# Three small VectorE operations per attention head, moved behind the first maximum of the next head

## The reference

```
x = x + 0.5 * ffn(layernorm(x))          # ternary weights, bias, gamma, beta
x = x + attn(layernorm(x))
x = x + 0.5 * ffn(layernorm(x))

attn:  q, k, v = x @ w.T, by heads;  q, k = rope(q), rope(k)
       scores = q k^T / sqrt(32), masked (causal by blocks of 64)
       softmax over keys, times v, then @ w_o.T
```

## Time and profile before

| | |
|---|---|
| median of 3 runs | 636.81 us (636.68 to 638.52) |
| profiled execution | 636.18 us, span of the trace 634.4 us |
| TensorE matmul busy | 554.8 us (87%), 3586 matmuls |
| VectorE busy | 409.6 us (65%), 782 instructions |
| ScalarE busy | 310.5 us (49%), 629 instructions |
| GpSimd busy | 238.9 us (38%), 200 instructions |
| chain that ended last | PE 69%, DVE 23%, issue 3%, ACT 2% of the span |
| granted TensorE clock, mean | 0.968 |

### The profile page before, as it was taken

How to read it: one execution, slowest core, us unless ns; L and a number is a source line. 1 busy time by engine, 2 the same in 40 slices (tenths; PEclk the granted TensorE clock), 3 DMA queues, 4 the chain that set the end, 5 groups by cost and what they waited for, 6 DMA issues and landing times.

```text
span 634.4 us, 10072 instructions
## 1 busy us (share of the span) xinstructions
PE 554.8 (87%) x3586; PEld 235.4 (37%) x3586; DVE 409.6 (65%) x782; ACT 310.5 (49%) x629; POOL 238.9 (38%) x200
## 2 busy tenths in 40 slices
PE   0785799679878999999999999999999898998866
PEld 0542545334323333333333333333344233343432
DVE  5999656626878668667677677677667822522462
ACT  0831622122215756756756666666656456661320
POOL 4001454443656547547556556556500100100100
PEclk9897899899979999999999999999999999999897
DMA  9930022363222125323123126323410021101011
GB/s 313 355 118 25 2 74 92 116 154 123 76 75 76 52 77 175 118 76 109 52 77 107 58 76 208 97 81 119 133 36 2 2 80 71 50 6 55 8 67 66
DMA packets 43602, 57.95 MB, mean 91 GB/s; under 512 B 3527, under 2 KB 34375, under 8 KB 42529
## 3 DMA queue, kind: packets, MB, share of 16 engines
q1 hardware_dynamic: 42972, 57.21, 27.5%
q10 hardware_dynamic: 580, 0.11, 0.1%
HBM read 32.01 MB, written 25.17 MB: 90 GB/s over the span
## 4 chain that ended last, share of the span: by engine, by line
PE 69%; DVE 23%; issue 3%; ACT 2%; DMA 1%; POOL 1%; SPq 0%; ACTq 0%; DVEq 0%; POOLq 0%
PE bank L956 11%; PE bank L1045 10%; PE bank L920 9%; PE bank L939 9%; PE bank L1055 8%; PE bank L874 7%; PE bank L884 6%; PE bank L993 5%; DVE rmax L815 5%; DVE stats L661 3%; DVE mparts L828 3%; DVE rmax L825 2%; PE bank L864 2%; DVE big L676 2%; DVE kst L676 1%
## 5 line engine op out<-in xcount | busy, mean ns | idle before, releaser
L815 DVE TENSOR_REDUCE rmax<-bank 128x1 f32<-128x512 f32 (+3 forms) x384 | 198.8, 551 | 107.7 <-PE bank L939 105.2
L609 ACT ACTIVATE big<-bank 128x512 f32<-128x512 f32 (+3 forms) x384 | 181.6, 492 | 141.9 <-PE bank L920 138.8
L939 PE MATMUL bank<-kst,qst 104*128 104x512 f16 (+3 forms) x384 | 126.2, 331 | 23.0 <-DVE rmax L815 16.4
L920 PE MATMUL bank<-qst,kst 106*128 106x512 f16 (+3 forms) x384 | 125.8, 329 | 3.1 <-ACT big L609 2.8
L502 POOL TENSOR_TENSOR rot<-t,sin_s 64x512 f32<-64x512 f32 x64 | 82.1, 1282 | 92.5 <-ACT t L602 89.8
L1045 PE MATMUL bank<-big,ones 128*32 128x512 f32 (+3 forms) x768 | 81.8, 498 | 0.0
L1055 PE MATMUL bank<-big,rows 128*32 128x512 f32 (+3 forms) x768 | 79.5, 486 | 0.0
L920 PEld LDWEIGHTS bank<-qst,kst 106*128 106x128 f16 x384 | 36.9, 96 | 89.9 <-issue 39.3
L511 POOL TENSOR_TENSOR rhl<-t,rhl 128x512 f16<-128x512 f32 x32 | 37.5, 1172 | 70.0 <-ACT rhl L623 70.0
L939 PEld LDWEIGHTS bank<-kst,qst 104*128 104x128 f16 x384 | 37.9, 99 | 64.2 <-DVE rmax L815 22.8
L956 PE MATMUL bank<-xh,wh 128*128 128x512 f16 x128 | 50.3, 393 | 6.3 <-DVE xl L697 5.9
(11 more groups left out here) (106 smaller groups left out, 688.6 us busy)
## 6 DMA issues: line engine op xcount, KB each, us to landing
spread<-rhl SPq DMA_DIRECT2D x32, 256.0 KB, 2.2
qst<-spread SPq DMA_DIRECT2D x16, 384.0 KB, 3.8
kst<-spread SPq DMA_DIRECT2D x16, 384.0 KB, 3.9
x<-rows SPq DMA_DIRECT2D x4, 1024.0 KB, 4.6
spread<-rhl SPq DMA_DIRECT2D x32, 128.0 KB, 2.1
rows<-in_L_attn_x_dram SPq DMA_DIRECT2D x3, 1024.0 KB, 15.4
xh<-ch SPq DMA_DIRECT2D x4, 512.0 KB, 5.5
xl<-cl SPq DMA_DIRECT2D x4, 512.0 KB, 6.7
```

What stands on the lines that cost most here:

```text
L609: nc.scalar.activation(probs[:, st % P_PLACES, h, 0:n], pb[u % 2][:, 0:n], ACT.Exp, scale=EXP_SCALE).then_inc(s_eb, 1)
L815: nc.vector.tensor_reduce(rmax[:, at:at + 1], a_bank(u)[:, 0:n], AX.X, ALU.max, negate=True).then_inc(s_max, 1)
L920: nc.tensor.matmul(pb[u % 2][:, 0:n], kst[0:ROWS_B, g % SETS, h, j * P:(j + 1) * P], qst[0:ROWS_B, g % SETS, h, q0:q0 + n], start=True, st ...
L939: nc.tensor.matmul(a_bank(u)[:, 0:n], qst[0:ROWS_A, g % SETS, h, i * P:(i + 1) * P], kst[0:ROWS_A, g % SETS, h, half * HALF:half * HALF + ...
```

## The change

The condition on the step in which VectorE issues the three small operations goes from lag 0 to lag 1, that is, from the step of a head's twelfth unit to the next step. Nothing else in the kernel is edited.

```diff
                 if (o := o_unit(k, 1) or o_late(k, 1)) and o[2] == 5:
                     attention_update(o[0], o[1])
-                if e := max_head(k, 0):
+                if e := max_head(k, 1):
                     n = GH * e[0] + e[1]
                     s, at = n % 2, A_UNITS * (n % HEADS)
                     dve.wait_ge(s_max, A_UNITS * (n + 1))
                     if n >= 2:
                         dve.wait_ge(s_mtr, n - 1)
                     link(nc.vector.tensor_tensor(rmax[:, at + 4:at + 8], rmax[:, at + 4:at + 8],
                                                  rmax[:, at + 8:at + 12], ALU.min))
```

## The result

The changed kernel takes 628.21 us (median, 628.06 to 628.44), the kernel before in the same series 637.66 us. The ratio is 0.985 with a 95% interval of 0.9827 to 0.9873: faster by 9.6 us, between 8.1 and 11.0. The profiled execution has a span of 626.6 us against 634.4, 7.8 us less. The forecast was 629.3 us and 7.5 us of gain.

A forecast was written before the change was run, and what follows sets the result against it. TensorE was taken to set the pace, idling mainly for maxima. Six pairs 6.1, heads 0 and 1 1.2, head 30 0.5, less 0.3 for the clock, made 7.5 us: 629.3 us on the median, range 623 to 634.5.

The forecast's parts named there:

- M1' right behind M12, small operations unmoved: End of a head on VectorE: M1' ends near 285.0 instead of 287.19 at head 12, small operations still at 286.99.
- The cover that I named: First GpSimd rotation, head 12: leaves 0.65 us of room after M1', so line 825's delay of 0.1 to 0.2 costs nothing.
- 0.48 and 0.53 per pair: Heads 12 and 13: S5' starts 0.48 and 0.53 us earlier, the rest becoming a shorter wait for M2'.
- the six pairs: Heads 4 and 5, 8 and 9, to 24 and 25: 1.01 us gained per pair, 6.1 us in all.
- Heads 0 and 1: S4' can come 0.62 us earlier at each, 1.2 us for both, with no new wait; 0.9 if overlap is no gain.
- Heads 2 and 3: Gain swallowed at head 4's wait for the second half of k, behind a DMA to `kst`: 0, at most 1 us.
- Head 30: Normalizations, then M1', without the small operations ahead: S4' gains 0.3 to 1.0 us, taken as 0.5.
- as I had feared: Head 30: GpSimd is at work there too, so a first normalization may stand in the small operations' stead.
- the forecast's clock term of -0.3: Half-speed stretch at 182.5 to 189.4 us: gives back 0.6 if it stays, nothing if it moves along; taken as 0.3.
- All idle time goes: Rival: M2' is not held up, S4' and S5' come earlier by the whole wait; 13.5 us gained, 623.3 us; chance 0.10.
- The wait only moves: Rival: S4' is freed but S5' or something later waits as before; gain under 1.9 us, 635 to 637; chance 0.12.
- A lost slot: Rival: small operations end one 1.3 us GpSimd operation later, at all heads or none; 21 us lost, 658 us; chance 0.05.

The follow-up runs named there:

- e1: Kernel before, with the move only at the ends of twelve heads (4, 5, 8, 9, to 24, 25): 630.93 us, ratio 0.990 to the kernel before.
- e3: Changed kernel, with GpSimd beginning three of every four ropes only after the small operations: 619.52 us, ratio 0.9722 to the kernel before.
- e2: Changed kernel, with the small operations one place further back, behind M2' (lag 2): 632.8 us, ratio 0.9935 to the kernel before.
- e5: Kernel before, with the move at all heads but 4, 5, 8, 9, to 24, 25: 635.81 us, ratio 0.9965 to the kernel before.
- e6: As e3, but GpSimd holds back the fourth rope of a group too: 623.15 us, ratio 0.9784 to the kernel before.
- e4: Kernel before (lag 0), with GpSimd beginning three of every four ropes only after the small operations: 621.89 us, ratio 0.9766 to the kernel before.

## Why the prediction was right

**M1' right behind M12, small operations unmoved.** At head 12 M1' ran 0.61 to 0.89 us after M12's start, line 825 started 0.81 instead of 0.72 after it, and line 828 ended at 2.90 instead of 2.89. The cover that I named, the first rotation, took the delay whole. VectorE's busy time fell from 409.6 to 405.1 us, mostly since line 825 stands for a shorter time (712 to 628 ns in the mean), which I had not counted.

**0.48 and 0.53 per pair.** The ruler gives 11.28 to 10.82 and 11.46 to 10.95: 0.46 and 0.51. The new waits at S5' are 0.18 and 0.34 us. For the six pairs 6.1 were forecast; e1 alone gave 5.9 in heads 4 to 26.

**Heads 0 and 1.** 1.2 forecast, 1.26 found (10.66 to 10.03, twice), with no new wait.

**Heads 2 and 3.** Forecast 0, since a DMA to `kst` is what head 4 waits for the earlier trace rows. From M12 of head 2 to that matmul it was 14.04 us before and 13.89 after. Here the freed time did turn into waiting: TensorE's idle time ahead of it went from 2.45 to 4.34 us. What the part still gained, 1.2 us in all, is nearly all clock: 0.15 of it comes before that matmul. Two stages of the changed kernel, 487 to 492 us and 183 to 188 us; the last three figures are clock, DMA share and GB/s:

```profile
487.00:492.00 5.00, 4.28 (x20) 0.92 (x21) 5.00 (x10) 1.12 (x2) 2.17 (x2) 0.66 0.00 0
183.00:188.00 5.00, 3.75 (x12) 1.38 (x13) 1.98 (x4) 0.79 (x2) 1.63 (x2) 0.66 0.02 4
```

At the start of head 4 a mean clock of 0.66 over 5 us makes 3.4 us at half speed, where 0.51 over 6.9 us had made 6.8, so part of what I had booked as a loss of 0.3 was a gain of about 1.

**Head 30.** Forecast 0.5. In the changed kernel heads 30 to 31 took 13.85 instead of 13.38 us, 0.5 longer, and the rows above show why: the granted clock fell to half near 488 us, when TensorE had just idled 1.79 us for a maximum that stood behind VectorE's statistics. Before, the same wait was there (1.78 us) and the clock stayed full. VectorE and TensorE of e3, where the clock stayed full too:

```profile
482.92 0.68 DVE L817 TENSOR_REDUCE rmax<-bank 128x1 f32<-128x512 f32 x1
483.52 2.44 DVE L678 TENSOR_SCALAR qst<-rows,mv,rstd 128x512 f32<-128x512 f32 x4
485.88 0.28 DVE L817 TENSOR_REDUCE rmax<-bank 128x1 f32<-128x128 f32 x1
```

```profile
486.21 0.39 PE L941 MATMUL bank<-kst,qst 104*128 104x512 f16 x1 [0.36 <-DVE rmax L817]
...
487.09 0.38 PE L941 MATMUL bank<-kst,qst 104*128 104x512 f16 x1
```

There, and in e2, heads 30 to 31 take 12.78 us: 0.60 better than before. The wait at S4' fell from 0.96 to 0.36 us; the first normalization stood for GpSimd, as I had feared (2.44 for the four instead of 1.91). So the term was right at full clock, and the clock took it back, with 1.07 us (13.85 less 12.78). Beside the half-speed stretch the order made next to no difference there: 13.85 to 13.89 us at lag 1 (changed kernel, e5, e6), 13.89 at lag 0 (e1, e4).

**What I missed.** At heads 7, 11, 15 and 23 the ruler gives 0.10 to 0.16 us each, 0.5 in all, though no wait of S4' stands in the list. At the end of head 15 it is S4' that comes 0.15 us earlier against M12 (3.14 instead of 3.29), and the idle time ahead of its weight load falls from 0.28 to 0.04 us; so it had most likely been held by M1' as well. At head 19 the changed kernel lost 0.27 us, as the first of the two DMA hops to `kst` landed 0.8 us later there than at the other heads and S5' waited 0.48 us; the kernel before has a trace of it at the same head (11.41 instead of 11.19). I did not find out what delays them.

**The sum.** In the profiles: 1.26 (heads 0 and 1), 1.20 (heads 2 and 3, mostly clock), 6.14 (heads 4 to 26), -0.48 (to head 31), 1.24 (after it) and -1.59 (before head 0, where nothing was changed) make 7.8. The 1.24 after head 31 go with the clock too, in the last feed-forward step, where the mean clock over 8 us was 0.57 before and 0.79 after:

```profile
619.00:627.00 8.00, 6.65 (x18) 2.44 (x19) 1.39 (x2) 0.57 (x1) 0.00 (x0) 0.57 0.09 33
...
613.00:621.00 8.00, 7.18 (x26) 2.95 (x27) 2.08 (x3) 0.04 (x1) 0.00 (x0) 0.79 0.09 33
```

What can be traced to the moved maxima is 1.26 + 0.15 + 6.1, so 7.5 us, against 7.3 forecast without head 30. That part was right for the reason given. That the span as a whole came out at 7.8 is partly luck: about 1 us of clock gained at head 4, 1.2 gained after head 31, 1.1 lost at head 30 and 1.6 lost before head 0 nearly cancel, and the forecast's clock term of -0.3 had only the first of them, with the wrong sign. The timed medians differ by 9.45 us, 1.7 more than the profiled executions (636.18 and 628.44), because the one of the kernel before lay 1.5 under its median and the other 0.2 above. Why is not shown. The runs of the kernel before go from 634.3 to 639.7 us over all series with mean clocks of 0.957 to 0.973, those of the changed kernel from 628.06 to 628.44, all at 0.973.

**The rivals.** All idle time goes: no, S5' waits. The wait only moves: at heads 2 and 3 alone. A lost slot: not at lag 1, but shown at lag 2, though not at all heads or none, as I had argued: 23 of the 27 lost one. (TensorE's share in the earlier trace rows is 96.4%, not the 97 I gave there; nothing hangs on it.) SBUF — State Buffer of the Trainium skill, "Who interferes with whom", has the operation that issues second stand until the first is over. By that rule, the trace agrees: at head 12 line 828 takes 1.11 us beside a rotation and 0.17 in e3, where the rotation starts after it.

## What to carry to other kernels

When a tiny operation takes a microsecond, look at what the other engine runs beside it and where that ends: here it stood until the neighbour's operation ended, so a small shift was free until it crossed such a boundary, and then cost about a slot of 1.3 us at most heads. Moving the work that others wait for ahead of such a block gives what the next consumer in the rotation leaves free, not the whole wait; one wait_ge that holds the neighbour back for 1.3 us gave almost as much again (e3, 619.52 us, the fastest version). Before calling a chain of DMAs full, check whether its stages start when their input comes or in a fixed later step.

## What the runs showed of the hardware

- Beside GpSimd operations of 1.3 us, VectorE operations on 4 to 8 numbers per partition took up to 1.21 us (line 825 at head 4 of e2), and 0.15 to 0.17 without. It struck all three, the one with a single tensor input (line 827, 1.13 us at head 0 of e2) too. Maxima read from PSUM (line 815) were not lengthened: in the kernel before one over 256 keys took 0.41 us at 287.11, beside GpSimd, and 0.43 at 463.35, with GpSimd idle.
- The granted clock fell to half near head 30 in the changed kernel, e1, e4, e5 and e6, and stayed full in the kernel before, e2 and e3, at the same work and with the same idle time of 1.8 us ahead of it. Where it fell, heads 30 to 31 took 1.07 us longer at lag 1 (13.85 against 12.78) and 0.51 at lag 0 (13.89 against 13.38). What decides it, these runs do not show.
